# A Mamba block and a mixture of experts in one kernel: the statistics of z and the copies of last states on ScalarE, every engine's order rearranged

## The chip, the cores and the metric

The kernel runs on one core of a Trainium2 chip. Times are device microseconds (us) of one execution. A core has five engines that work through their own instructions in order and meet only at semaphores: TensorE (PE, with its weight loads as PEld), VectorE (DVE), ScalarE (ACT), GpSimd (POOL) and SyncE (SP, which issues all transfers here).

## The reference, cut to what matters

Four batches of 512 positions. Each goes through a selective state-space layer with 512 channels and 16 states per channel, gated by the layer-normed `x`, and then through a layer of 8 experts (the best 2 are weighted) and one shared expert.

```python
u = silu(causal_conv(in_proj_w @ ctx) + conv_b)
dt_lo, B, C = split(x_proj_w @ u)
delta = softplus(dt_proj_w @ dt_lo + dt_proj_b)
# for every position t
state = state * exp(delta_t * A) + delta_t * u_t * B_t
y_t = sum_over_states(state * C_t)
z = layernorm(x)                      # over 512
x = x + tanh(g_xattn) * (y + D * u) * silu(z)
n = layernorm(x)
top2 = top_k(softmax(n @ gate_w.T), 2)
h = gelu(n @ wd.T + bd) * weight_of_expert
x = x + tanh(g_ffn) * (h @ wu + bu + gelu(n @ ws_d.T + bs_d) @ ws_u.T + bs_u)
```

## The kernel before

**Units and slots.** The batches are cut into six units (`UNITS`): unit 0 and 1 are the halves of batch 0 (256 positions each), units 2 and 3 are batches 1 and 2 whole (512), units 4 and 5 the halves of batch 3. The recurrence of a unit is cut into slots, 128 in all: 16 in units 0, 1, 4 and 5, 32 in units 2 and 3. So unit 1 begins at slot 16, unit 2 at 32, unit 3 at 64, unit 4 at 96, unit 5 at 112. A slot holds 32 channels times 4 groups of states on 128 partitions and 1024 elements of states and positions. Four slots (`r` = 0 to 3) make up a group of 128 channels.

**One slot.** SP loads `dd` (delta and delta times u, spread over partitions). POOL multiplies by B for two slots at once into `ring` (`outers`, L988). ScalarE writes exp(delta A) into one of two PSUM buffers `decay` (`exps`, L1064), and may do so once the scan of two slots earlier, or its weighing, is done. VectorE runs the recurrence (`scan`, L1229). The multiplication by C is POOL's for r = 0 and 1 (`weigh`, L1010, two slots at once) and VectorE's for r = 2 and 3 (L1243, the result of the scan stays in `decay` until then). When a batch goes on in the next unit (units 0 and 4), the last states of a slot are copied into `carry`: by POOL for r = 0 and 1 (L1006), by VectorE for r = 2 and 3 (L1235, between scan and weighing). PE then sums over the states into `y_ps` (L1458; called y0.0 and so on: unit, then group). VectorE gates it with z (L1280), POOL adds the residual (L964). `ring` has ten buffers, so POOL's products for slot i wait until the sums up to slot i minus 10 are done.

**Preparation of a unit.** PE `in_proj` (L1474), ScalarE and VectorE the convolution (L1089, L1255, L1257), ScalarE SiLU (L1095), PE `x_proj` and `dt` (L1482, L1487), ScalarE softplus (L1115, with table loads around it), POOL delta times u (`du`, L957), SP's store and loads of `dd`.

**Statistics of z.** For each batch VectorE takes four times `bn_stats` and `bn_aggr` (L1270, L1272), POOL makes scale and shift of them (`affine_z`, L946 to L951), ScalarE applies SiLU (`silu_z`, L1099).

**The expert layer of a unit.** Means and variances over the channels by PE (`mean_p`, `mean`, `var_p`, `var`), centring and scaling by VectorE (L1305, L1311), the routing (L1344 to L1397), nine `down` jobs (L1523), read by ScalarE (L1163) and put through GELU in two pieces (L1170), eight `mix` jobs (L1527) that VectorE multiplies in (L1404), four `up` jobs (L1531, L1537) that VectorE reads (L1409). All these PE jobs share three PSUM banks `wk` in turn: a job waits until the bank's last reader is done. In this document "down5.0" is the first down job of unit 5.

**What sets the order.** Each engine's order is written down in the table `PLAN`: a number for each piece of work, in slots. PE and SP work through theirs sorted by number. On POOL, ScalarE and VectorE a piece is issued ahead of the slot whose number it has before the point, and the slots themselves follow a fixed loop. Nothing is decided at run time, and an engine that waits for one piece holds back all behind it.

## Time and profile before

| | us |
|---|---|
| median of 3 runs | 643.73 |
| the three runs | 643.26, 643.73, 643.81 |
| the profiled execution, its own time | 644.75 |
| its span, from the first instruction to the last | 643.0 |
| busy: PE, VectorE, POOL, ScalarE | 502.3, 505.0, 494.2, 396.6 |

The busy times are shares of the whole span, which has three parts: about 36 us until the first scan, the 128 slots until about 576 us, and an end of about 65 us in which PE works through the rest of the expert layers while POOL and, mostly, VectorE have nothing left. So an engine that is busy for 490 us is near its limit in the middle part. The profile attributes idle time to what ended it; where several semaphores are awaited that is the last one.

### The profile page before, as it was taken

To read this page: it belongs to the slowest core of one execution; us is meant where nothing else is said; L and a number is where in the kernel's file an instruction comes from. 1 tells how busy PE (TensorE), PEld (TensorE's weight loads), DVE (VectorE), ACT (ScalarE), POOL (GpSimd) and SP (SyncE) were. 2 spreads that over 40 slices of the span, in tenths; PEclk is the share of its full clock that TensorE was granted. 3 is DMA by queue.
4 is the path that set the end of the run, shared out by engine and by line. 5 is a ranking of instruction groups with operands and counts; after the bars stand their busy time and mean duration, and the time that the engine had idled before them with its cause. 6 is when DMAs were issued, how large, how long until landed. Compare 5 with 4: busy or idle time off the path is not lost.

```text
span 643.0 us, 7504 instructions
## 1 busy us (share of the span) xinstructions
PE 502.3 (78%) x2304; PEld 253.7 (39%) x2304; DVE 505.0 (79%) x560; ACT 396.6 (62%) x755; POOL 494.2 (77%) x240
## 2 busy tenths in 40 slices
PE   5605544787899698974399899974998999889988
PEld 4202211234564364610033333331443443657866
DVE  4477799878989999995879899958689879982211
ACT  4549656897926877474666854455689765681250
...
GB/s 83 166 371 210 255 66 99 115 249 166 97 150 184 63 196 2 106 113 304 244 95 7 130 79 110 27 240 201 50 49 41 208 181 123 25 2 67 33 1 49
DMA packets 39940, 79.70 MB, mean 124 GB/s; under 512 B 5977, under 2 KB 12761, under 8 KB 39900
## 3 DMA queue, kind: packets, MB, share of 16 engines
...
q8 instruction: 18, 0.29, 0.2%
q14 instruction: 22, 0.18, 0.1%
...
## 4 chain that ended last, share of the span: by engine, by line
DVE 34%; PE 27%; ACT 14%; issue 14%; POOL 7%; DMA 3%; ACTq 0%; DVEq 0%; SPq 0%; POOLq 0%
DVE decay L1229 11%; DVE ring L1229 8%; PE wk L1537 8%; PE wk L1523 7%; ACT decay L1064 5%; POOL ring L988 5%; DVE ring L1243 4%; PE y_ps L1458 3%; PE wk L1474 3%; DMA dd<-dd_scratch 2%; PE wk L1487 2%; ACT L1033 2%; POOL ring L1010 1%; DVE xc L1305 1%; ACT h L1163 1%
## 5 line engine op out<-in xcount | busy, mean ns | idle before, releaser
L988 POOL TENSOR_TENSOR ring<-dd,b_in 128x2048 f32<-128x2048 f32 x64 | 289.3, 4531 | 15.8 <-issue 13.1
L1064 ACT ACTIVATE decay<-dd,a_neg 128x255 f32<-128x255 f32 (+1 forms) x384 | 188.4, 533 | 37.3 <-DVE ring L1229 37.0
L1229 DVE TENSOR_TENSOR_SCAN ring<-decay,ring 128x1024 f32<-128x1024 f32 x64 | 144.4, 2277 | 16.1 <-ACT decay L1064 10.1
L1010 POOL TENSOR_TENSOR ring<-ring,c_in 128x2048 f32<-128x2048 f32 x32 | 144.9, 4527 | 13.1 <-DVE ring L1229 7.7
L1229 DVE TENSOR_TENSOR_SCAN decay<-decay,ring 128x1024 f32<-128x1024 f32 x64 | 146.3, 2285 | 8.5 <-ACT decay L1064 5.7
L1523 PE MATMUL wk<-xc,w_down 128*128 128x256 f32 (+1 forms) x432 | 139.4, 478 | 11.7 <-DVE xc L1311 6.0
L1537 PE MATMUL wk<-h,w_up 128*128 128x256 f32 (+1 forms) x432 | 137.2, 474 | 0.4 <-DVE h L1404 0.4
L1458 PE MATMUL y_ps<-ring,fold 128*32 128x256 f32 (+1 forms) x768 | 77.4, 547 | 64.3 <-DVE ring L1243 63.3
L1523 PEld LDWEIGHTS wk<-xc,w_down 128*128 128x128 f32 x432 | 84.3, 201 | 62.0 <-issue 46.6
L1537 PEld LDWEIGHTS wk<-h,w_up 128*128 128x128 f32 x432 | 84.3, 200 | 44.5 <-issue 35.1
L1243 DVE TENSOR_TENSOR ring<-decay,c_in 128x1024 f32<-128x1024 f32 x64 | 78.2, 1222 | 1.7
L1458 PEld LDWEIGHTS y_ps<-ring,fold 128*32 128x32 f32 x768 | 25.5, 127 | 109.2 <-DVE ring L1243 74.3
L1046 ACT ACTIVATE decay<-zeros 128x4 f32<-128x4 f32 (+1 forms) x64 | 10.9, 171 | 60.3 <-DVE ring L1243 60.2
L1474 PE MATMUL wk<-ctx_in,in_w 128*128 128x256 f32 (+2 forms) x96 | 40.4, 564 | 8.6 <-DMA ctx_in<-in_ctxT 6.3
L1163 ACT ACTIVATE h<-wk,b_down 128x256 f32<-128x256 f32 (+1 forms) x54 | 28.7, 538 | 26.3 <-PE wk L1523 26.2
L1409 DVE SCALAR_TENSOR_TENSOR x_out<-wk,consts,x_out 128x256 f32<-128x256 f32 (+1 forms) x24 | 13.5, 562 | 32.8 <-PE wk L1537 32.7
L964 POOL TENSOR_TENSOR x<-x,y_gated 128x256 f32<-128x256 f32 (+1 forms) x24 | 21.8, 910 | 18.4 <-DVE y_gated L1280 12.8
L957 POOL TENSOR_TENSOR dd_out<-dd_out,u 128x256 f32<-128x256 f32 (+1 forms) x24 | 21.4, 903 | 17.8 <-ACT dd_out L1115 17.6
L1404 DVE TENSOR_TENSOR h<-h,wk 128x256 f32<-128x256 f32 (+1 forms) x48 | 21.1, 501 | 14.1 <-PE wk L1527 13.1
L1487 PE MATMUL wk<-x_dbl,dt_w 16*128 16x256 f32 (+1 forms) x48 | 24.4, 630 | 9.9 <-DVE u L1255 5.6
L1255 DVE SCALAR_TENSOR_TENSOR u<-wk,conv_taps,u 128x255 f32<-128x255 f32 (+5 forms) x48 | 29.3, 613 | 3.6 <-ACT u L1089 2.4
L1474 PEld LDWEIGHTS wk<-ctx_in,in_w 128*128 128x128 f32 x96 | 21.0, 235 | 27.0 <-issue 20.4
...
## 6 DMA issues: line engine op xcount, KB each, us to landing
...
```

The lines of the kernel that those rows point to most:

```text
L988: nc.gpsimd.tensor_tensor(two, dd[:, j % DD_RING:j % DD_RING + 2, None, n:2 * n].broadcast_to([P, 2, TILES[v], n]), b_in[:, None, g % BC_R ...
L1010: nc.gpsimd.tensor_tensor(two, two, c_in[:, None, g % BC_RING].broadcast_to([P, 2, WIDE]), ALU.mult).then_inc(weighed_pool, 2)
L1064: last = nc.scalar.activation(decay[:, i % 2, q * n + 1:(q + 1) * n], dd[:, j % DD_RING, 1:n], ACT.Exp, scale=a_neg[:, c, r, k:k + 1])
L1163: nc.scalar.activation(h[:, k, columns(v)], wk[:, bank, 0:COLS[v]], ACT.Identity, bias=b_down[:, k:k + 1]).then_inc(drained[bank], 1)
L1229: last = nc.vector.tensor_tensor_scan(to, decay[:, i % 2], ring[:, i % RING], 0.0, ALU.mult, ALU.add)
L1243: nc.vector.tensor_tensor(ring[:, i % RING], decay[:, i % 2], c_in[:, g % BC_RING], ALU.mult).then_inc(weighed_dve, 1)
L1255: ins = nc.vector.scalar_tensor_tensor(to[:, d:], wk[:, bank, 0:n - d], tap, to[:, d:], ALU.mult, ALU.add)
L1458: last = nc.tensor.matmul(y_ps[r * BLOCK:(r + 1) * BLOCK, 0:n], fold[:], ring[:, slots[r] % RING, q * n:(q + 1) * n], start=False, stop=p ...
L1474: last = nc.tensor.matmul(wk[:, bank, 0:n + halo], in_w[:, j, k * P:(k + 1) * P], ctx_in[:, j, cols.start - halo:cols.stop], start=j == 0, ...
L1487: last = nc.tensor.matmul(o, dt_w[:, k * P:(k + 1) * P], x_dbl[0:R, 0:n], start=True, stop=True)
L1523: last = nc.tensor.matmul(o, w_down[:, j, k, :], xc[:, j, cols], start=j == 0, stop=j == NW - 1)
L1537: last = nc.tensor.matmul(o, w_up[:, j, k * P:(k + 1) * P], h[:, j, cols], start=False, stop=j == NE - 1)
```

## The change

Three things are changed.

1. **Statistics of z.** VectorE's `bn_stats` and `bn_aggr` go. ScalarE takes the sums by four copies of 128x512 in place with an accumulated sum (L1130 of after), the negative mean by one small copy (L1133), and the squares about the mean by eight squarings of 128x256 into a scratch tile with accumulated sums, each waiting for the one ahead (L1138). `affine_z` on POOL adds the two halves and divides; it has four small instructions as before.
2. **Copies of last states.** VectorE's copy for r = 2 and 3 goes, 16 in all. ScalarE makes it (`keep`) ahead of overwriting the `decay` buffer two slots later, so after the weighing; POOL's products of the next unit wait for it (`kept`).
3. **Order.** Every number of `PLAN` is new. Which instructions there are does not change by this. The identity matrix lies in `xc` during the constants' making, which frees memory for the scratch tile.

```diff
+Z_STEPS = 3 * NW + 1
     "z": [
-        [-1.66],
+        [-1.85],
...
-                pool.wait_ge(z_stats, 2 * NW * (b + 1))
+                pool.wait_ge(z_stats, Z_STEPS * (b + 1))
...
-                nc.gpsimd.tensor_tensor(z_ln[:, 0], z_mv[:, :, 1], eps.broadcast_to([P, NW]), ALU.add)
-                nc.gpsimd.tensor_tensor(z_ln[:, 1], z_mv[:, :, 0], minus_one.broadcast_to([P, NW]), ALU.mult).then_inc(z_scale, 1)
+                nc.gpsimd.tensor_tensor(z_ln[:, 0], z_var[:, :, 0], z_var[:, :, 1], ALU.add).then_inc(z_scale, 1)
+                pool.wait_ge(z_scale, 4 * b + 1)
+                nc.gpsimd.tensor_scalar(z_ln[:, 0], z_ln[:, 0], 1.0 / L, EPS, ALU.mult, ALU.add).then_inc(z_scale, 1)
...
+                    pool.wait_ge(kept, keeps(i + 1))
...
+            def keep(i):
+
+                v, c, p, r = PLACES[i]
+                if goes_on(v) and not weighs_on_pool(i):
+                    k, n = p * TILES[v], COLS[v]
+                    nc.scalar.activation(carry[:, c * NR4 + r, k:k + TILES[v], None],
+                                         decay[:, i % 2].rearrange("p (q n) -> p q n", n=n)[:, :, n - 1:n], ACT.Copy).then_inc(kept, 1)
...
+                    keep(i - 2)
                 reset(i)
+                if i > 1 and kept_of(i - 2):
+                    act.wait_ge(kept, kept_of(i - 2))
...
+            def stats_z(b, k):
+
+                pair = range(2 * (k % 2), 2 * (k % 2) + 2)
+                if k == 0:
+                    act.wait_ge(z_loaded, DMA * (b + 1))
+                    if b > 0:
+                        act.wait_ge(z_scale, 4 * b)
+                if k < 2:
+                    for c in pair:
+                        nc.scalar.activation(z[:, c, :], z[:, c, :], ACT.Copy, accum_out=z_sum[:, c:c + 1]).then_inc(z_stats, 1)
+                if k == 1:
+                    act.wait_ge(z_stats, Z_STEPS * b + NW)
+                    nc.scalar.activation(z_ln[:, 1], z_sum[:], ACT.Copy, scale=-1.0 / L).then_inc(z_stats, 1)
+                if k > 1:
+                    for c in pair:
+                        for half in range(2):
+                            act.wait_ge(z_stats, Z_STEPS * b + NW + 1 + 2 * c + half)
+                            nc.scalar.activation(z_scrap[:], z[:, c, half * L // 2:(half + 1) * L // 2], ACT.Square, bias=z_ln[:, 1, c:c + 1],
+                                                 accum_out=z_var[:, c, half:half + 1]).then_inc(z_stats, 1)
...
-                if goes_on(v) and not weighs_on_pool(i):
-                    steps[0] += 1
-                    last.then_inc(scan_step, 1)
-                    dve.wait_ge(scan_step, steps[0])
-                    k = p * TILES[v]
-                    last = nc.vector.tensor_copy(carry[:, j, k:k + TILES[v], None],
-                                                 to.rearrange("p (q n) -> p q n", n=n)[:, :, n - 1:n])
...
-                nc.vector.bn_stats(z_stat[:, c, :], z[:, c, :]).then_inc(z_stats, 1)
-                dve.wait_ge(z_stats, 2 * w + 1)
-                nc.vector.bn_aggr(z_mv[:, c, :], z_stat[:, c, :]).then_inc(z_stats, 1)
```

**Where rows move.** In the rows below a name such as `wk<-ctx_in,in_w` is what is written and what is read, the size is that of the output, and x8 stands for eight instructions in a row; what an instruction waits for stands in brackets.

The first place is the beginning of PE's order, before: `in_proj` of units 0 and 1 (`ctx_in`), `x_proj` (`xp_w`) and `dt` (`dt_w`) of unit 0, then the first sums.

```order
L1474 MATMUL wk<-ctx_in,in_w 128x256 x8
L1474 MATMUL wk<-ctx_in,in_w 128x259 x6
L1482 MATMUL wk<-u,xp_w 48x256 x4
L1487 MATMUL wk<-x_dbl,dt_w 128x256 x3
L1474 MATMUL wk<-ctx_in,in_w 128x259 x2
```

The same place after.

```order
L1498 MATMUL wk<-ctx_in,in_w 128x256 x8
L1506 MATMUL wk<-u,xp_w 48x256 x4
L1511 MATMUL wk<-x_dbl,dt_w 128x256
L1498 MATMUL wk<-ctx_in,in_w 128x259 x2
L1511 MATMUL wk<-x_dbl,dt_w 128x256 x3
```

Unit 1's `in_proj` (output 128x259) has moved behind `x_proj` and behind the first `dt`.

The second place is POOL between unit 3 and unit 4, before: from the last weighing of unit 3 (`c_in`) over `du` of unit 4 (`dd_out`) and unit 3's last residual (`x<-x,y_gated`) to unit 4's first products (`dd,b_in`) and `affine_z`.

```order
L1010 TENSOR_TENSOR ring<-ring,c_in 128x2048 [waits scanned,c_loaded2]
L957 TENSOR_TENSOR dd_out<-dd_out,u 128x256 [waits u_ready,drained2]
L957 TENSOR_TENSOR dd_out<-dd_out,u 128x256 [waits u_ready,drained0]
L957 TENSOR_TENSOR dd_out<-dd_out,u 128x256 [waits u_ready,drained1]
L957 TENSOR_TENSOR dd_out<-dd_out,u 128x256 [waits u_ready,drained0]
L964 TENSOR_TENSOR x<-x,y_gated 128x512 [waits gated]
L988 TENSOR_TENSOR ring<-dd,b_in 128x2048 [waits b_loaded0,dd_loaded5,summed,dd_loaded4]
L988 TENSOR_TENSOR ring<-dd,b_in 128x2048 [waits b_loaded0,dd_loaded1,summed,dd_loaded0]
L988 TENSOR_TENSOR ring<-dd,b_in 128x2048 [waits b_loaded0,dd_loaded3,summed,dd_loaded2]
L946 TENSOR_TENSOR z_ln<-z_mv,consts 128x4 [waits siluz_ready,z_stats]
```

The same place after, from the weighing but one of unit 3.

```order
L964 TENSOR_TENSOR dd_out<-dd_out,u 128x256 [waits u_ready,drained2]
L996 TENSOR_TENSOR ring<-dd,b_in 128x2048 [waits b_loaded0,dd_loaded5,summed,dd_loaded4]
L1018 TENSOR_TENSOR ring<-ring,c_in 128x2048 [waits scanned,c_loaded2]
L971 TENSOR_TENSOR x<-x,y_gated 128x512 [waits gated]
L996 TENSOR_TENSOR ring<-dd,b_in 128x2048 [waits b_loaded0,dd_loaded1,summed,dd_loaded0]
L971 TENSOR_TENSOR x<-x,y_gated 128x512 [waits gated]
L996 TENSOR_TENSOR ring<-dd,b_in 128x2048 [waits b_loaded0,dd_loaded3,summed,dd_loaded2]
L964 TENSOR_TENSOR dd_out<-dd_out,u 128x256 [waits u_ready,drained2]
```

Unit 4's first two products have moved ahead of unit 3's last residual, and its `du` are spread out: two are done before this place and in it, two come with the slots of unit 4.

The third place is the end of PE's order, before: from the sums of the last group, y5.3 (`y_ps<-ring,fold`), over unit 4's `up` (`w_up`) to unit 5's `down` (`w_down`) and `up`.

```order
L1458 MATMUL y_ps<-ring,fold 32x256 x16
L1527 MATMUL wk<-comb_parts,sel 128x256 x3
L1491 MATMUL wk<-x,consts 32x256 x4
...
L1531 MATMUL wk<-comb_parts,b_up 128x256
L1537 MATMUL wk<-h,w_up 128x256 x9
L1515 MATMUL wk<-ident,parts 48x128 x2
L1523 MATMUL wk<-xc,w_down 128x256 x28
L1527 MATMUL wk<-comb_parts,sel 128x256 x8
L1531 MATMUL wk<-comb_parts,b_up 128x256
```

The same place after.

```order
L1482 MATMUL y_ps<-ring,fold 32x256 x16
L1547 MATMUL wk<-xc,w_down 128x256 x8
L1515 MATMUL wk<-x,consts 32x256 x4
L1547 MATMUL wk<-xc,w_down 128x256 x4
...
L1547 MATMUL wk<-xc,w_down 128x256 x4
L1551 MATMUL wk<-comb_parts,sel 128x256 x3
L1555 MATMUL wk<-comb_parts,b_up 128x256
L1561 MATMUL wk<-h,w_up 128x256 x9
L1551 MATMUL wk<-comb_parts,sel 128x256 x5
L1555 MATMUL wk<-comb_parts,b_up 128x256
```

Four `down` jobs of unit 4 (16 matmuls) now stand behind y5.3, and unit 4's last `up` job stands between the third and the fourth `mix` job (`sel`) of unit 5.

## Rows read from the trace of the kernel before

**Rows 1.** the page: the chain that ended last, by engine.

```profile
DVE 34%; PE 27%; ACT 14%; issue 14%; POOL 7%; DMA 3%; ACTq 0%; DVEq 0%; SPq 0%; POOLq 0%
```

**Rows 2.** busy time by stretch: start:end, length, five engines, PE clock granted, DMA.

```profile
36.50:102.40 65.90, 24.66 (x148) 9.90 (x148) 57.22 (x52) 42.66 (x95) 62.88 (x31) 0.66 0.58 204
...
170.20:305.00 134.80, 110.48 (x528) 59.73 (x526) 122.01 (x131) 82.99 (x138) 119.40 (x38) 0.86 0.39 132
305.00:421.70 116.70, 100.33 (x353) 36.97 (x352) 109.54 (x96) 70.47 (x113) 109.17 (x33) 0.91 0.29 99
421.70:441.60 19.90, 11.46 (x46) 3.89 (x46) 12.76 (x23) 10.05 (x19) 15.37 (x6) 0.67 0.87 299
...
514.50:577.80 63.30, 57.62 (x364) 31.36 (x363) 55.87 (x58) 43.37 (x106) 55.61 (x31) 0.97 0.25 84
577.80:643.00 65.20, 59.77 (x271) 45.43 (x270) 15.12 (x46) 15.41 (x24) 0.73 (x1) 0.95 0.11 37
```

**Rows 3.** instructions by line and form: count, busy us, mean ns, idle before.

```profile
L988 POOL TENSOR_TENSOR ring<-dd,b_in 128x2048 f32<-128x2048 f32 x64 | 289.3, 4531 | 15.8 <-issue 13.1 <-DMA dd<-dd_scratch 2.7
...
L1270 DVE BATCH_NORM_STATS2 z_stat<-z 128x6 f32<-128x512 f32 x16 | 10.8, 672 | 0.0
...
L1272 DVE BATCH_NORM_AGGREGATE z_mv<-z_stat 128x2 f32<-128x6 f32 x16 | 2.9, 182 | 0.6
L1235 DVE COPY carry<-decay 128x4 f32<-128x4 f32 x16 | 2.6, 162 | 0.6
```

**Rows 4.** timeline of the beginning: start, length, engine, line, instruction, idle before.

```profile
22.62 1.22 PE L1487 MATMUL wk<-x_dbl,dt_w 16*128 16x256 f32 x2 [3.88 <-DVE u L1257]
23.88 0.47 ACT L1115 ACTIVATE dd_out<-wk,dt_bias 128x256 f32<-128x256 f32 x1 [3.28 <-PE wk L1487]
...
31.97 4.50 POOL L988 TENSOR_TENSOR ring<-dd,b_in 128x2048 f32<-128x2048 f32 x1 [1.36 <-DMA dd<-dd_scratch]
```

**Rows 5.** timeline on VectorE around the first statistics of z.

```profile
40.89 0.67 DVE L1270 BATCH_NORM_STATS2 z_stat<-z 128x6 f32<-128x512 f32 x1
...
44.07 2.28 DVE L1229 TENSOR_TENSOR_SCAN decay<-decay,ring 128x1024 f32<-128x1024 f32 x1
```

**Rows 6.** instructions by line and form on ScalarE.

```profile
L1033 ACT ACT_TABLE_LOAD x24 | 30.8, 1283 | 0.4
...
L1099 ACT ACTIVATE z<-z,z_ln 128x512 f32<-128x512 f32 x16 | 11.7, 803 | 4.9 <-POOL z_ln L951 4.8
...
L1095 ACT ACTIVATE u<-u 128x256 f32<-128x256 f32 x16 | 5.3, 401 | 0.0
...
L1170 ACT ACTIVATE h<-h 128x2560 f32<-128x2560 f32 x2 | 4.7, 2341 | 0.0
...
L1095 ACT ACTIVATE u<-u 128x512 f32<-128x512 f32 x8 | 4.4, 616 | 0.0
```

**Rows 7.** timeline between unit 3 and unit 4.

```profile
427.49 1.27 POOL L964 TENSOR_TENSOR x<-x,y_gated 128x512 f32<-128x512 f32 x1 [3.21 <-DVE y_gated L1280]
...
428.71 13.50 POOL L988 TENSOR_TENSOR ring<-dd,b_in 128x2048 f32<-128x2048 f32 x3
...
441.62 2.27 DVE L1229 TENSOR_TENSOR_SCAN ring<-decay,ring 128x1024 f32<-128x1024 f32 x1
...
453.76 2.30 DVE L1229 TENSOR_TENSOR_SCAN decay<-decay,ring 128x1024 f32<-128x1024 f32 x1 [4.03 <-ACT decay L1064]
```

**Rows 8.** timeline of the end, on PE.

```profile
604.03 12.46 PE L1523 MATMUL wk<-xc,w_down 128*128 128x256 f32 x56
...
620.78 6.68 PE L1537 MATMUL wk<-h,w_up 128*128 128x256 f32 x18 [0.36 <-DVE h L1404]
...
627.60 4.15 PE L1537 MATMUL wk<-h,w_up 128*128 128x256 f32 x18
```

**Rows 9.** busy time by stretch at the end.

```profile
620.80:627.50 6.70, 6.70 (x19) 5.20 (x19) 0.00 (x1) 0.00 (x0) 0.00 (x0) 0.62 0.00 0
627.50:640.40 12.90, 12.84 (x57) 10.20 (x56) 1.47 (x4) 0.00 (x0) 0.00 (x0) 1.00 0.16 51
```

572 lines of the change are left out of this document (285 added, 287 removed), and 77 rows, old and new, of the table PLAN.

## The prediction

> **What bounds the kernel now.** I read four views in this order: the page's chain, the busy time by stretch, the groups of instructions, and the timeline where the change moves something. In the chain no engine leads: VectorE has 34%, PE 27%, ScalarE 14%, issue 14% and POOL 7% [rows 1]. The stretches [rows 2] say where each one counts. In unit 0 POOL is busy 62.88 of 65.9 us and VectorE 57.22. In unit 2 it is VectorE, 122.01 of 134.8, with POOL at 119.40; in unit 3 they are level, 109.54 and 109.17 of 116.7. In unit 5 PE is the busiest, 57.62 of 63.3, VectorE and POOL just behind. In the last 65.2 us PE alone counts, 59.77. ScalarE is the bound in none of them, at 57% to 69% of a stretch. Between units 3 and 4 there is a hole: from 421.7, where the slots of unit 3 are through, to the next scan at 441.62 [rows 2, 7] nobody is full. That is 19.9 us without a scan.
>
> The profiled execution took 644.75, 1.02 above the median of 643.73. I add up differences on its span of 643.0 and apply the sum to the median; that both scale alike is an assumption, and 0.16% of the sum is nothing. About 0.2%, or 1.3 us, is what a measurement of this kernel can tell from no change.
>
> **Part 1, the statistics.** VectorE is rid of 16 times 672 plus 182 ns [rows 3], 13.7 us, 3.4 for each batch; by the starts of the first statistics and of the scan behind them, 40.89 and 44.07, a set takes 3.2 [rows 5]. ScalarE gets four copies of 128x512, a small one and eight squarings of 128x256 for each batch, all with an accumulated sum, which no row shows. Bounds for the copy: 616 ns is 128x512 with a plain scale, 803 the one with two operands per partition [rows 6]; for the squaring 401 from below [rows 6] and, since every one waits for the one ahead and stores its sum, 401 plus 162 plus a wait, say 0.7, from above. I take 0.75 and 0.55: 4 x 0.75 + 0.2 + 8 x 0.55 = 7.6 for each batch, 30 in all (bounds 23 and 37). So the same work costs ScalarE over twice what VectorE saves. It is free where ScalarE has slack over the slots around it, as in unit 2 (83 of 134.8 busy), and it is not where a set stands as a block ahead of an `exps`: there are only two `decay` buffers, so ScalarE is never more than two slots ahead.
>
> The trace has ScalarE's 128x512 at 616 to 803 ns against VectorE's pair at 854, so per instruction there is no loss; it is the second pass that doubles the cost. The Trainium skill, "ScalarE: Activation LUTs", section "Rules for kernel authors", tells one to put adds and multiplies on VectorE and not on ScalarE, which speaks against this part. Its section "What ACT_TABLE_LOAD costs" gives 186 + 0.833 N ns with immediates and some 93 more per pointer operand: as an estimate 0.61 for the copy and 0.49 for the squaring, 6.4 a batch instead of my 7.6, with no figure for the accumulated sum. By that price the sum stays at 634.2, since I count the statistics as hidden; by the rule as written the part would be a loss, the rival further down that gives 650. No row here shows either yet.
>
> **Part 2, the copies of last states.** VectorE loses 16 times 162 ns and the wait for the scan's end ahead of each, together some 3.3 us, all in units 0 and 4 [rows 3]. ScalarE gets 16 small ones in place of them, about 0.2 each. They come ahead of overwriting `decay`, two slots later, for which the weighing had to be finished anyway, so they add no wait but only their length and that of the semaphore behind them: 0.3 to 0.5 us in a slot of about 4 (134.8 us for 32 slots in unit 2 [rows 2]). POOL's wait for them comes at the next unit's products, long after. I put the part at nothing by itself; it counts in what VectorE gains below.
>
> **Part 3, the order, by stretch.** *Beginning and unit 0.* PE's first `dt` stood 3.88 us waiting for a bank that VectorE's convolution of unit 1 held [rows 4]: unit 1's `in_proj` had been queued ahead of it. Now it comes behind, so the softplus (which had waited 3.28 for PE), the store and POOL's first product follow earlier: 31.97 becomes about 28, if the wait of 1.36 for the transfer stays [rows 4]. Unit 0 is bound by POOL, whose work in it does not change, so the gain is carried through to slot 16. Next in line is the first set of statistics: it now takes 7.6 of ScalarE between two `exps` where VectorE lost 3.2, and may eat some of the gain. I take **-4.0**, bounds -5.5 and 0.
>
> *Units 1 to 3.* Unit 2 gives VectorE 3.2 back, and its slack is 134.8 - 122.0 = 12.8, POOL's 15.4: both engines have idle time from waits on each other, so the gain can't be larger than what VectorE loses plus some of these. I take **-3.0**, bounds -4.5 and +1.5 (the last when ScalarE's 7.6 hold an `exps`). In unit 3 VectorE also loses 3.2 us of statistics, but gets part of unit 5's convolution, about as much, so 0; unit 1 gets no statistics before or after: 0.
>
> *The hole.* POOL waits 3.21 us for the gate of unit 3's last group, y3.7, takes the residual (1.27) and only then three products, 13.5 us [rows 7]; the first scan of unit 4 needs the first of them, and the loads of unit 4 (DMA busy share 0.87 in this stretch [rows 2]) had to be there. VectorE meanwhile has 12.76 us of other work [rows 2], mostly a convolution, a centring and statistics that stand there in one lump. After, the first products of unit 4 are ahead of the last residual, in part before unit 3's last weighing, and `dt` and convolution are spread over the units on either side. If everything then were ready, the next scan could follow within a slot (about 4 us) instead of 19.9: the upper end is -16. But the work of the stretch is still to be done: VectorE's 12.76 less 3.2 of statistics, POOL's 15.37, ScalarE's 10.05 plus 7.6 for statistics [rows 2]. Where it's put now, in slots 96 to 108, ScalarE is the one that is full: softplus for unit 5, its table loads of 1283 ns each, silu(z) at 803 x 4 and the statistics come in the same eight or nine slots. Even so slot 108 should come some 14 us sooner. At slot 112 both pieces of unit 4's GELU are now near each other, each with a table load ahead and one behind: twice 1.28 + 2.34 + 1.28 = 9.8 at most [rows 6], and the reads of the down jobs beside them. `exps` of slots 113 to 116 wait for that, with VectorE's and POOL's work behind them; this gives back about 9. That leaves -5; POOL, which enters unit 5 with less behind it (55.61 of 63.3 busy, so 7.7 to spare), gives 2 more. I take **-7.0**, bounds -16 and -1. The wait for `decay` shows today already, 4.03 us in one slot of unit 4 [rows 7]; it is what is late next.
>
> *The end.* From the last group y5.3 on, PE is the bound. Unit 5's last four down jobs have been moved behind it. 56 records, seven jobs, take 12.46, so 1.78 each [rows 8]: 7.1, and with `comb` and three mixes about 8.2 of PE work that used to run beside the slots. Against this, unit 4's last `up` now stands between the mixes of unit 5 and covers the wait for the last GELU. There PE had been idle enough for the granted clock to fall: the up job at 620.78 took 6.68 at a granted 0.62 (near 1.2 GHz through much of it), the one at 627.60 took 4.15 at 1.00 (2.4 GHz) [rows 8, 9]. Keeping the clock gives 2.5, the waits about 1.2. Net **+4.5**, bounds +2 (PE has only 5.7 us to spare in unit 5, so these jobs were not wholly hidden before and give part of it back there) and +8.4 (nothing of the clock and the waits is saved).
>
> **The sum.** -4.0 - 3.0 - 7.0 + 4.5 = -9.5. On the median: 643.7 - 9.5 = **634.2**. All low ends together would give 620, all high ones 653. Half of each distance, added in squares since the terms are independent, is 4.8 downward and 4.7 upward: the forecast's own range is 629 to 639.
>
> **Rivals.**
> *The hole closes nearly entirely.* ScalarE's extra in slots 96 to 108 is taken up in its slack (31% to 43% idle in the stretches above), the bunch at slot 112 costs 3 and not 9, and the sum gains 6 to 8 more: 627. For it: ScalarE idles 9.85 of 19.9 us in the hole [rows 2]. Against: its work stands in lumps, and there are two buffers only.
> *POOL sets the pace and VectorE's relief is worth nothing.* POOL does 64 products of 4.53 us [rows 3], none less after, and is at 89% to 95% in units 0, 2 and 3 [rows 2]. What the hole gains by starting early is then lost again before slot 112, because POOL's products there are as many as before. What is left is the beginning, -4.0, and the end at its upper value, +8.4, less perhaps 1 to 3 of the hole: **646**, slower. It decides if POOL's idle time between slot 96 and y5.3 shrinks by less than 4 us.
> *ScalarE becomes the bound.* If statistics and copies cost their upper bounds (37 + 8 = 45 us) and two thirds of a set are each time ahead of an `exps` that VectorE awaits, four sets cost 4 x 5 = 20, VectorE's 3.2 x 4 come back only if it isn't waiting, and the order's gain of 14 is used up: about **650**. Against: ScalarE's 57% to 69%. In this case the rule of the Trainium skill that is named above, in "ScalarE: Activation LUTs", would prove right.
> *The change does only half of it:* the hole halves, the end gives it back, and the time is within 1.3 of before, 643.7.
>
> **Chances.** Forecast 0.55; the hole closes 0.18; POOL 0.13; ScalarE 0.06; the half-done change 0.08. So faster by over 0.2%: 0.73; within 0.2%: 0.08; slower by over 0.2%: 0.19. The range for 8 in 10 reaches from 624, which holds most of the larger gain, to 646, which ends at POOL's case and leaves ScalarE's out.
>
> **What would show it.** *Beginning:* POOL's first product near 28, no wait of PE ahead of the first `dt`, slot 16 near 98.5. *Statistics:* ScalarE's busy time up by 30, to some 428, VectorE's down by 16, to about 489; squarings near 0.55 and copies near 0.75. *Hole:* the first scan of unit 4 within 5 us of the last slot of unit 3, then scans that wait for `decay`; another, shorter standstill after slot 112. *End:* y5.3 to the end about 70 us instead of 65, with the last up jobs all at 4.15 and clock 1.00. I am wrong if the time up to slot 96 does not drop by 5 to 8 us, if the wait for `decay` grows beyond some 25 us over the whole run, or if the end grows by more than 8.

## The result, and the profile after

The changed kernel took 625.3 us (median of 4 executions, 617.63 to 629.19), against 643.77 before (643.26 to 644.36). These medians stand 18.5 us apart, a ratio of 0.971; the two quicker of the four, 617.63 and 622.23, count as fast runs and alone give 0.963 (95% interval 0.957 to 0.969). Six more executions gave 626.33 (623.04 to 628.71) against 643.9, ratio 0.972 (0.970 to 0.975). So the change makes the kernel some 18 us faster, nearly twice the 9.5 that was forecast. That is below the forecast's own range of 629 to 639, and just inside the low end of the one for 8 in 10, 624 to 646. The changed kernel also scatters over 11.6 us in its first four executions and 5.7 in the six, where the one before stays within 4.2 in eleven. The profile shown is that of the quickest of the six, 623.04 us with a span of 621.3, so some 4 us of the 21.7 between the two spans are scatter.

Busy time by stretch, with the same borders as [rows 2]: unit 0, unit 1, unit 2, unit 3 up to slot 92, slots 92 to 112, unit 5 up to the end of y5.3, the end.

```profile
37.50:96.40 58.90, 26.85 (x160) 10.71 (x160) 51.77 (x37) 49.41 (x123) 57.44 (x27) 0.67 0.68 226
96.40:160.40 64.00, 46.81 (x284) 25.00 (x284) 60.26 (x67) 55.16 (x122) 62.41 (x34) 0.85 0.41 140
160.40:282.30 121.90, 105.95 (x480) 60.21 (x484) 113.72 (x112) 88.55 (x160) 119.90 (x38) 0.83 0.43 147
282.30:394.40 112.10, 96.48 (x338) 35.11 (x330) 101.05 (x91) 79.01 (x142) 106.85 (x33) 0.85 0.36 126
394.40:490.00 95.60, 85.25 (x397) 35.02 (x396) 76.66 (x78) 77.33 (x170) 79.45 (x40) 0.95 0.37 127
490.00:547.90 57.90, 54.41 (x298) 27.02 (x296) 52.90 (x44) 34.36 (x89) 51.08 (x27) 0.97 0.30 101
547.90:621.30 73.40, 67.12 (x312) 51.31 (x308) 18.01 (x61) 23.51 (x36) 0.72 (x1) 0.97 0.10 33
```

Three stretches of the kernel before that [rows 2] do not show by themselves: unit 1, unit 3 up to slot 92, and slots 92 to 112.

```profile
102.40:170.20 67.80, 53.91 (x282) 27.48 (x282) 57.05 (x60) 56.09 (x119) 64.13 (x34) 0.76 0.50 168
305.00:411.00 106.00, 90.54 (x309) 33.10 (x309) 98.88 (x89) 64.32 (x104) 99.32 (x28) 0.90 0.31 106
411.00:514.50 103.50, 86.55 (x352) 35.33 (x351) 83.09 (x97) 73.72 (x138) 77.86 (x38) 0.85 0.36 123
```

The chain that ended last, against [rows 1]:

```profile
PE 30%; DVE 26%; ACT 19%; issue 16%; DMA 4%; POOL 3%; SPq 1%; DVEq 0%; ACTq 0%; POOLq 0%
```

ScalarE has 19% of it instead of 14%, VectorE 26% instead of 34%. In unit 2 POOL is busy 119.90 of 121.9 us; it was 119.40 of 134.8 [rows 2]. POOL's work in it has hardly changed, its idle time is nearly gone. The prediction's terms side by side with the lengths of the stretches:

| stretch | before | after | change | forecast |
|---|---|---|---|---|
| until the first scan, and unit 0 | 36.5 + 65.9 | 37.5 + 58.9 | -6.0 | -4.0 |
| unit 1 | 67.8 | 64.0 | -3.8 | 0 |
| unit 2 | 134.8 | 121.9 | -12.9 | -3.0 |
| unit 3 up to slot 92 | 106.0 | 112.1 | +6.1 | 0 |
| slots 92 to 112 (the hole, and what follows) | 103.5 | 95.6 | -7.9 | -5.0 |
| slot 112 to y5.3 | 63.3 | 57.9 | -5.4 | -2.0 |
| the end | 65.2 | 73.4 | +8.2 | +4.5 |
| sum | 643.0 | 621.3 | -21.7 | -9.5 |

A second profile of the changed kernel, of an execution of 628.36 us with a span of 626.6, tells scatter from effect. There the first two rows are -2.5 and -2.8, unit 2 -14.1, unit 3 up to slot 92 +4.8, slots 92 to 112 -4.8, and all from slot 112 on +3.0. Unit 2 stands out in both; the size of the head's gain does not hold.

ScalarE's `exps` and VectorE's scans by line, then the new instructions on ScalarE by line and form (count, busy us, mean ns, idle before):

```profile
L1088 ACT ACTIVATE decay<-dd,a_neg 128x255 f32<-128x255 f32 (+1 forms) x384 | 188.4, 533 | 27.7 <-DVE ring L1271 27.4
L1271 DVE TENSOR_TENSOR_SCAN decay<-decay,ring 128x1024 f32<-128x1024 f32 x64 | 145.8, 2285 | 15.8 <-ACT decay L1088 14.5
...
L1138 ACT ACTIVATE z_scrap<-z,z_ln 128x256 bf16<-128x256 f32 x32 | 16.2, 506 | 0.9
L1130 ACT ACTIVATE z<-z 128x512 f32<-128x512 f32 x16 | 9.8, 616 | 0.2 <-DMA z<-in_x 0.2
L1138 ACT ACTIVATION_READ_ACCUMULATOR z_scrap<-z,z_ln 128x1 f32 x32 | 6.0, 187 | 0.0
L1130 ACT ACTIVATION_READ_ACCUMULATOR z<-z 128x1 f32 x16 | 3.0, 187 | 0.0
L1067 ACT ACTIVATE carry<-decay 128x4 f32<-128x4 f32 x16 | 2.6, 162 | 8.1 <-DVE ring L1278 8.1
```

An accumulated sum is an instruction of its own, 187 ns, that overlaps its neighbour a little. A set from 38.4 to 46.1 us (in the run head_fix3) is 7.7 us, the 7.6 of the prediction; ScalarE's busy time rose from 396.6 to 426.2, VectorE's fell from 505.0 to 488.5. These terms were right in size. For the set that is in part luck: from start to start a copy with its sum takes 0.61 us where 0.75 was taken, and a squaring with its sum 0.64 where 0.55 was, and the two errors cancel.

### The profile page after: what moved, and what is told of

It reads as the page before. It is cut to its first block, busy times and chain, and to the rows that moved or that the text cites. A ratio compares the mean times of both kernels' runs of the same rounds, so it can differ in the third digit from the quotient of the medians.

```text
span 626.6 us, 7564 instructions
## 1 busy us (share of the span) xinstructions
PE 499.8 (80%) x2304; PEld 253.7 (40%) x2304; DVE 487.9 (78%) x512; ACT 426.5 (68%) x872; POOL 494.0 (79%) x240
## 4 chain that ended last, share of the span: by engine, by line
DVE 30%; PE 29%; ACT 17%; issue 13%; DMA 7%; POOL 3%; SPq 1%; DVEq 0%; ACTq 0%; POOLq 0%
DVE ring L1271 10%; DVE decay L1271 9%; PE wk L1547 8%; PE wk L1561 8%; ACT decay L1088 5%; DVE ring L1278 3%; PE y_ps L1482 3%; DMA dd<-dd_scratch 3%; DVE u L1290 2%; POOL ring L996 2%; PE wk L1511 2%; ACT z_scrap L1138 2%; PE wk L1523 2%; PE wk L1498 2%; PE wk L1506 2%
## 5 line engine op out<-in xcount | busy, mean ns | idle before, releaser
L1088 ACT ACTIVATE decay<-dd,a_neg 128x255 f32<-128x255 f32 (+1 forms) x384 | 188.4, 533 | 27.2 <-DVE ring L1271 26.9
L1561 PE MATMUL wk<-h,w_up 128*128 128x256 f32 (+1 forms) x432 | 134.9, 468 | 1.6 <-DVE h L1430 1.5
L1561 PEld LDWEIGHTS wk<-h,w_up 128*128 128x128 f32 x432 | 82.4, 195 | 45.4 <-issue 36.6
L1482 PE MATMUL y_ps<-ring,fold 128*32 128x256 f32 (+1 forms) x768 | 73.3, 523 | 11.3 <-POOL ring L1018 5.7
L1506 PE MATMUL wk<-u,xp_w 128*48 128x256 f32 (+1 forms) x48 | 20.7, 590 | 25.7 <-ACT u L1119 24.7
L964 POOL TENSOR_TENSOR dd_out<-dd_out,u 128x256 f32<-128x256 f32 (+1 forms) x24 | 21.8, 914 | 21.3 <-ACT dd_out L1159 21.2
L1498 PEld LDWEIGHTS wk<-ctx_in,in_w 128*128 128x128 f32 x96 | 21.7, 240 | 31.5 <-issue 17.4
```

The costliest lines, as they stand in the source:

```text
L1088: last = nc.scalar.activation(decay[:, i % 2, q * n + 1:(q + 1) * n], dd[:, j % DD_RING, 1:n], ACT.Exp, scale=a_neg[:, c, r, k:k + 1])
L1482: last = nc.tensor.matmul(y_ps[r * BLOCK:(r + 1) * BLOCK, 0:n], fold[:], ring[:, slots[r] % RING, q * n:(q + 1) * n], start=False, stop=p ...
L1498: last = nc.tensor.matmul(wk[:, bank, 0:n + halo], in_w[:, j, k * P:(k + 1) * P], ctx_in[:, j, cols.start - halo:cols.stop], start=j == 0, ...
L1506: last = nc.tensor.matmul(o[0:R + 2 * NS, :], xp_w[:, j, :], u[:, (NW * v + j) % U_RING, 0:n], start=j == 0, stop=j == NW - 1)
L1561: last = nc.tensor.matmul(o, w_up[:, j, k * P:(k + 1) * P], h[:, j, cols], start=False, stop=j == NE - 1)
```

## Experiments: order and engines apart

**The changed kernel again**, unchanged.

> The changed kernel again, unchanged: its four runs so far lie between 617.6 and 629.2, at mean granted TensorE clocks from 0.895 down to 0.861, where the kernel before stays within 1 us. If the clock is what spreads them, the runs go on lying on one line of time against clock (about 3 us for 0.01) and the profile of a quicker run shows the same stretches until some stretch in which PE is the busiest, with a higher granted clock there. If it is something else (transfers, POOL), the clock would be the same over quick and slow runs in the stretches that differ.

Measured: 626.33, six executions at mean granted clocks from 0.865 to 0.871, with times from 623.04 to 628.71 that do not follow the clock. The first four had followed it, from 617.63 at 0.895 to 629.19 at 0.861. So the clock as a whole does not explain the scatter of the six, and for the first four that is open. Two profiles, 626.6 and 621.3 long, differ by 1.6 us at slot 0, by 3.8 at slot 8, by 1.7 to 5.9 from there to slot 108 and by 5.1 at slot 112. In the longer one PE's clock was 0.62 against 0.70 in the stretch from 39 to 75 us, and VectorE waited 2.1 us for a y's sums (0 in the other). What starts it was not tried.

**The order alone.** The code of before with the new `PLAN`.

```diff
 PLAN = {
-    (numbers of before)
+    (numbers of the changed kernel)
 }
```

> Kernel before with the numbers of the changed kernel's table and nothing else: statistics and copies stay on VectorE. Theory 1 (the order is the gain, POOL's 15 us of idle time in unit 2 and the hole are what closes): -12 to -18 against before, about 628. Theory 2 (VectorE's relief is the gain, the order only serves it): -2 to -6, about 640, since VectorE is given 16 us back in places where it is full.

Measured: 630.70 (630.04 to 632.68), ratio 0.980 (0.977 to 0.982), -13.2. Three quarters of the gain need no change of engines. By stretches: unit 0 58.5, unit 1 64.5, unit 2 122.6, unit 3 up to slot 92 115.0, slots 92 to 112 98.6. Against the changed kernel it lacks mainly 2.9 and 3.0 us in the last two.

**The engines alone.** The changed code with the numbers of before.

> Changed kernel with the numbers of the table of before: statistics and copies on ScalarE, old order. Theory 1 (order): within 3 us of before, 641 to 646, as the lump of VectorE at slot 35 only moves to ScalarE, whose four pieces of 7.6 us stand ahead of an exps. Theory 2 (VectorE's relief): -8 or more, below 636. Theory 3 (statistics on ScalarE hurt where they stand in one slot): slower than before by 3 to 10.

Measured: 679.33 (678.71 to 681.16), ratio 1.055 (1.052 to 1.058): 35 us slower than before. None of the theories had that. By the slots' starts it is lost in four places, where the sets stand: 4.8 us in slots 0 to 4, 5.9 in 32 to 36, 5.9 in 64 to 68 and 15.1 in 92 to 100. ScalarE's waits in the stretch around slot 35, and its timeline before slot 96:

```profile
ACT z L1128 <- DMA z<-in_x: 5.5, 1, 5.5
```

```profile
454.67 0.63 ACT L1128 ACTIVATE z<-z 128x512 f32<-128x512 f32 x1 [10.47 <-DMA z<-in_x]
```

VectorE, in the same kernel around slot 96 and around slot 35:

```profile
456.49 1.52 DVE L1290 SCALAR_TENSOR_TENSOR u<-wk,conv_taps,u 128x256 f32<-128x256 f32 x3 [9.73 <-ACT u L1111]
460.94 1.52 DVE L1290 SCALAR_TENSOR_TENSOR u<-wk,conv_taps,u 128x256 f32<-128x256 f32 x3 [2.93 <-ACT u L1111]
467.63 1.52 DVE L1290 SCALAR_TENSOR_TENSOR u<-wk,conv_taps,u 128x256 f32<-128x256 f32 x3 [5.17 <-ACT u L1111]
```

```profile
197.11 2.32 DVE L1288 SCALAR_TENSOR_TENSOR u<-wk,conv_taps,u 128x511 f32<-128x511 f32 x3 [11.40 <-ACT u L1111]
```

ScalarE runs up to two slots ahead of VectorE. With the same slot number it meets the statistics earlier, when z is not loaded yet, and waits 5.4 us in slot 2, 5.5 in slot 35, 10.5 in slot 96, with its reads of PE's banks and its `exps` queued behind. VectorE then waits for those reads. In the kernel before VectorE, which comes last, took the same statistics without any wait for the transfer.

The third set is different. ScalarE meets it in slot 67 with z already there, and does it as one block of 7.7 us. The reads of the means' chain stand behind it, and VectorE waits for them with its scans behind. ScalarE and VectorE there:

```profile
319.69 0.61 ACT L1128 ACTIVATE z<-z 128x512 f32<-128x512 f32 x1
```

```profile
336.83 2.29 DVE L1335 TENSOR_TENSOR xc<-xc,wk 128x2048 f32<-128x2048 f32 x1 [10.64 <-ACT wk L1180]
```

In the kernel before VectorE waited 1.51 us at this place. So the block costs 5.9 us here with no transfer awaited.

**The statistics spread.** As the engines alone, with the four pieces of a set in different slots.

```diff
-stats_z: 2.2 2.4 2.6 2.8 | 35.5 35.625 35.75 35.875 | 67.286 67.429 67.571 67.714 | 96.667 96.75 96.833 96.917
+stats_z: 2.2 2.6 3.2 3.6 | 35.5 36.5 37.5 38.5 | 65.5 66.6 67.5 68.5 | 96.9 97.2 98.1 98.5
-affine_z: 0.667 | 36.5 | 66.5 | 98.5
+affine_z: 2.5 | 39.5 | 68.6 | 98.5
```

> As engines_alone (679.3), but the four pieces of each set of statistics stand in two to four slots instead of in one, and POOL's affine_z behind them. If the block of 7.6 us between two exps is what costs (4.7 to 5.9 us in slots 0 to 4, 32 to 36, 64 to 68 and 12 to 15 around slot 96 in the run of engines_alone), a third to two thirds of the 35 us come back: 655 to 668. If the price is ScalarE's 30 us as such or POOL's wait for affine_z, nothing comes back: 675 to 682.

Measured: 673.47 (672.11 to 674.66), ratio 1.044, -5.9 of the 35, between the two expectations. Slots 32 to 36 came back to 22.5 us from 28.7 (before: 22.8), although ScalarE still waited for z there:

```profile
186.12 0.63 ACT L1128 ACTIVATE z<-z 128x512 f32<-128x512 f32 x1 [5.85 <-DMA z<-in_x]
```

Slots 64 to 68 came back to 21.2 from 26.4 (before: 20.5). So in slots 32 to 36 the block was what cost. In 64 to 68 that is less sure, since a long wait had moved just ahead of them: the third set's first piece, now in slot 65, waited 12.4 us for z, with the read that unit 4's convolution needs behind it, and slots 60 to 64 took 28.7 us instead of 20.4. ScalarE's waits for z grew from 21.4 us in all to 29.6, so the total does not measure the block alone.

**The statistics later, still in a block.**

```diff
-stats_z: 2.2 2.4 2.6 2.8 | 35.5 35.625 35.75 35.875 | 67.286 67.429 67.571 67.714 | 96.667 96.75 96.833 96.917
+stats_z: 3.3 3.5 3.7 3.9 | 37.6 37.7 37.8 37.9 | 68.7 68.8 68.9 68.95 | 98.1 98.3 98.5 98.7
-affine_z: 0.667 | 36.5 | 66.5 | 98.5
+affine_z: 4.2 | 38.5 | 68.6 | 98.6
```

> As engines_alone (679.3), but each set of statistics stands later in ScalarE's order, where z has been loaded, still as one block in one slot: slots 3, 37, 68 and 98 instead of 2, 35, 67 and 96. In engines_alone ScalarE waited 5.4, 5.5 and 10.5 us for the transfer of z with all its exps behind, in engines_spread 12.4 at slot 65. If these waits are most of the price, 650 to 662. If the block of 7.6 us itself is, it stays at 670 to 680.

Measured: 668.12, ratio 1.036 (1.033 to 1.038), -11.2 (-13.1 between the two profiles). Slots 32 to 36 took 18.6 us, 10.1 less than with the engines alone, and slots 92 to 96 took 32.2 against 42.6. The wait for z was 0.4 us there instead of 5.5, and 4.0 instead of 10.5. But in the head the set now met another wait: ScalarE stood 7.3 us for POOL's `affine_z` ahead of SiLU, slot 4 came at 65.1 instead of 61.0, and slots 0 to 4 took 5.0 us more. Slots 64 to 68, where there had been no wait for z, stayed at 27.2. So where the waits for the load shrank, 20.5 us came back, and 7.4 were lost elsewhere, 5.0 of them to the next wait in the head. Load and block do not add up: in slots 32 to 36 either edit alone took the whole loss away. The shares of the two in the 35 us stay open.

**The statistics back on VectorE**, in the new order.

> Changed kernel with the statistics back on VectorE as before, copies on ScalarE, new order. Theory 1: +1 to +5 against the changed kernel (VectorE 13.7 us more, of which most lies in its idle time). Theory 2: +8 to +14. If ScalarE's 30 us are the costlier place: 0 or faster than the changed kernel.

Measured: 629.54, ratio 0.978 (0.975 to 0.980), +3.2 against the changed kernel, as theory 1 had it. With the order alone at 630.70, the copies of last states are worth some 1.2 us, no more than the scatter. That the statistics gain 3 us in this order and stand among the losses in the old one fits their places: here z is there when ScalarE comes (a wait of 0.2 us in all), and three of the four sets are spread over two to four slots.

## Experiments: where the order gains

**The new order from a slot on.** Three kernels with the code of before; an entry keeps its old number if both numbers lie below the border.

> Code of before (statistics and copies on VectorE); every entry of the table whose number is below 20 in both tables keeps before's number, all others get the changed kernel's. By the starts of the slots in the run of the new order alone (-5.2 us at slot 16, -1.4 at slot 20, -13.6 at the end), the part up to slot 20 gives next to nothing: 630 to 634. If the head's gain counts in full, it is lost here: about 636.

> The same with the border at 45. The slots say that the order gains 16 us between slots 20 and 44. If these are independent of what follows, they are lost here and the later order by itself gives +3 to +6 against before: 647 to 650. If the later order gains by itself, through the hole, as the prediction had it (-7 and +4.5): about 641.

> The same with the border at 65, so the order of before up to unit 3, then the new one: the hole between units 3 and 4 closes, unit 3 and slots 100 to 112 get longer, the end gets longer. By the slots of the order alone against before from slot 64 on (345.1 against 338.0 us): +7, so about 650. The prediction's terms for this part, -7.0 and +4.5, would give 641.

Measured: 653.44, 645.56 and 645.02 (ratios 1.015, 1.000 and 1.001). From 65 on, the stretches from slot 64 to 92, 92 to 112, and from there to the end:

```profile
299.90:413.70 113.80, 92.90 (x322) 33.93 (x314) 103.71 (x99) 71.17 (x114) 106.61 (x33) 0.85 0.34 120
413.70:512.10 98.40, 86.55 (x396) 35.30 (x395) 81.18 (x93) 69.75 (x138) 79.21 (x40) 0.93 0.35 124
512.10:643.80 131.70, 121.87 (x605) 78.28 (x603) 70.91 (x104) 58.00 (x124) 52.08 (x28) 0.97 0.19 63
```

Slot 64 comes 5.0 us sooner than before, slot 96 16.6 sooner: the hole is closed. But unit 3 up to slot 92 takes 113.8 us against 106.0, and slot 112 comes only 2.4 sooner; the end takes that and 0.8 more. From slot 64 on it is 343.9 us against 338.0. Closing the hole is worth nothing by itself in this kernel: its work is in the slots on either side. The border at 20 has a fault of its own: ahead of slot 20 a centring waits 15.9 us for PE, whose means wait for a residual that POOL does late, and 20 us are lost. But from there on the pieces add up to the microsecond: slots 20 to 64 take 169.8 us, with the whole new order 169.4, before 188.7; from slot 64 on it is 345.1 in both. So the order's gain is made in unit 1 and unit 2, 19 us, the first 20 slots give 1.4, and all from unit 3 on costs 7. Of unit 2's 134.8 us 129.1 are left with the border at 65, 130.1 at 45, 122.6 with the whole: some 5 are saved by what is moved out of its end into unit 3, the rest by what is ordered below 45. The kernels with borders at 45 and 65 end level with before, within 0.2%. Their expectations had 647 to 650 and about 650, or 641 by the theory of the hole, so both are misses. Which rows of the order make the gain in units 1 and 2 was not found: none of the single moves that follow brings it.

**One place at a time, in the kernel before.** VectorE's lumps at slots 35 and 44:

```diff
-stats_z: 35.5 35.625 35.75 35.875    affine_z: 36.5
+stats_z: 36.6 37.6 38.5 39.6         affine_z: 40.5
-shares: 44.75    comb: 44.42    comb read: 46.5
+shares: 46.25    comb: 46.1     comb read: 47.45
```

> Kernel before with two groups of VectorE's work in unit 2 spread and nothing else: the statistics of batch 1 from slot 35 over slots 36 to 39 (POOL's affine_z behind them), and the end of the routing of unit 1 with its PE job from slot 44 to 46. If the lumps are what unit 2 loses (a scan 9.4 us late at slot 35, 7.7 us of POOL idle before slot 44), unit 2 shrinks by 4 to 8 us from 134.8, and the total by as much less what comes back later: 637 to 641. If VectorE's load as such is the bound in unit 2, nothing changes: 643 to 645.

Measured: 653.47, 9 us slower. Slot 36 came no sooner: VectorE waited for PE's up jobs there, 2.1 and 1.6 us, where it had waited 2.0 us and then done the statistics in the kernel before. So the lump had filled time that is idle without it. The loss itself came in slots 44 to 48, 7.6 us: ScalarE, which reads `comb` in its order ahead of an `exps`, stood still for PE:

```profile
243.66 0.38 ACT L1154 ACTIVATE comb_parts<-wk 48x256 bf16<-48x256 f32 x1 [7.90 <-PE wk L1512]
```

The weighing ahead of the routing (`weigh_d` 44.5 to 44.1), and the reads of unit 0's up jobs a slot later (`up read` 35.375, 36.333, 37.5 to 36.05, 36.6, 37.7, SP's transfers likewise):

> Kernel before with one number changed: VectorE's weighing in slot 44 stands ahead of the routing of unit 1 (13 small instructions, 2.9 us) and not behind it. In the trace of before, the weighing at 227.3 releases the exps at 228.7, their end at 230.0 releases SP's load, and that POOL's product at 233.9, which POOL had waited 7.7 us for. If this chain is what POOL waits for, the wait shrinks by 2 to 3 us to about 5, and slot 48 comes 2 to 3 us sooner; total 641 to 643. If POOL waits for something else, nothing changes (643.3 to 645).

> Kernel before with three of VectorE's four reads of unit 0's up jobs put a slot later (behind the scan of slot 35), and SP's transfers for them. In the trace of before, the first read waited 2.0 us for PE ahead of that scan, and with the convolution and the statistics the scan came at 189.3 where the one ahead had begun at 177.6. If the read's place costs, slots 36 to 40 come 2 to 4 us sooner: 640 to 642. If the wait only moves to the next scan or to PE (its banks are held longer), 643 to 647.

Measured: 644.16 and 643.81 against 644.82, ratios 0.999 (0.998 to 1.001) and 0.999 (0.998 to 1.000), so no difference that can be told. With the weighing first POOL waited 8.0 us there instead of 7.7: ScalarE's `exps` stood behind the routing's exponential and the reads of down jobs, not behind the weighing. With the reads later slot 36 came 3.5 us sooner as expected, and slot 64 still 1.8, but 1.3 of both were there at slot 32, ahead of the edit.

The gate at the border of units 2 and 3:

```diff
-gate y2.7: 64.5    conv 4.3: 64.75    residual 2.3: 62.5
+gate y2.7: 66.5    conv 4.3: 66.6     residual 2.3: 64.5
```

(the last of the four columns each; the residual is that of y2.7)

> Kernel before with three numbers changed: VectorE's gate of y2.7 and the convolution of unit 4's last 128 channels stand behind the scans of slots 64 and 65 and not ahead of them, POOL's residual behind one more product. In the trace of before the first scan of unit 3 began at 304.96, though POOL's product and ScalarE's exps were there by 299.7: VectorE waited 3.77 us for PE's sums and 0.87 for ScalarE's read, and did 2.3 us of work. If that is the cause, slot 64 comes 4 to 5 us sooner. If the gain lasts, the total is 639 to 641; if the wait is met again behind (PE's means wait for this residual), slot 72 shows less than 1 us of it and the total is 643 to 645.

Measured: 648.69, ratio 1.005 (1.004 to 1.007). Slot 64 came 3.5 us sooner, slot 68 2.8 later, slot 84 5.3 later. VectorE in this kernel behind the first scans of unit 3:

```profile
305.89 0.73 DVE L1277 SCALAR_TENSOR_TENSOR y_gated<-y_ps,consts,z 128x512 f32<-128x512 f32 x1
312.12 2.29 DVE L1302 TENSOR_TENSOR xc<-x,wk 128x2048 f32<-128x2048 f32 x1 [5.51 <-PE wk L1496]
```

The gate feeds the residual, that PE's means, and the centring, number 66.5 on VectorE as before, waited 5.5 us for them with all scans behind it. The gain moved from one wait into a longer one. The changed kernel moves the whole chain at once: `mean read` to 67.667, `scale_x` to 70.5, the statistics to 70.7 and later.

The residual on which the prediction laid the hole (number 92.875 to 94.5):

> Kernel before with POOL's last residual of unit 3 behind unit 4's first product instead of ahead of it. The prediction held that this residual (3.2 us of waiting for the gate, 1.27 of work) keeps unit 4's first scan late. If so, slot 96 comes 3 to 4.5 us sooner than 441.6 and the total drops by 1 to 4. If VectorE's lump of other work (12.8 us of the 19.9) is what keeps it late, slot 96 does not move, and the chain of means starts later: total 644 to 648.

Measured: 648.36, ratio 1.005 (1.003 to 1.006). POOL's product began at 425.98 instead of 428.71, but the first scan of unit 4 came at 445.14, 3.5 us later than before. VectorE ahead of it:

```profile
427.94 1.53 DVE L1254 SCALAR_TENSOR_TENSOR u<-wk,conv_taps,u 128x256 f32<-128x256 f32 x3 [0.17 <-ACT u L1086]
436.34 1.52 DVE L1254 SCALAR_TENSOR_TENSOR u<-wk,conv_taps,u 128x256 f32<-128x256 f32 x3 [6.87 <-ACT u L1086]
438.26 2.29 DVE L1302 TENSOR_TENSOR xc<-x,wk 128x2048 f32<-128x2048 f32 x1 [0.40 <-PE wk L1496]
...
445.14 2.27 DVE L1226 TENSOR_TENSOR_SCAN ring<-decay,ring 128x1024 f32<-128x1024 f32 x1
```

It was never the product that was awaited. The queue of convolutions, centring and statistics ahead of the scan was, and in it the chain over residual and means.

**What takes the hole's gain back.** Half of unit 3's down jobs:

```diff
-for j in range(NW):
+for j in range(2 if v == 3 else NW):
     last = nc.tensor.matmul(o, w_down[:, j, k, :], xc[:, j, cols], ...)
```

> Changed kernel with the work of unit 3's nine down jobs halved (two of the four blocks of channels are left out, 18 matmuls of 128x512, some 16.6 us of PE). It asks why the hole that was closed between units 3 and 4 is paid back in slots 100 to 112, where PE is busy 95% in the changed kernel. If PE is the bound there, slot 112 comes 8 to 15 us sooner and the total falls by about as much. If ScalarE (table loads, GELU, softplus) or the chain from the last residual over the means to the first down job is the bound, slot 112 moves by under 4 us.

Measured, one execution: 626.61; slots 100 to 112 took 71.3 us against 70.3, where 8 to 15 less were expected if PE is the bound. PE is not the bound there, though it is 92% busy. Its records say why less work hardly left idle time: from 467 to 490 us, with the down jobs halved on the first row and whole on the second (the changed kernel),

```profile
467.00:490.00 23.00, 18.66 (x99) 6.57 (x98) 17.63 (x15) 20.07 (x37) 20.97 (x11) 0.72 0.25 88
```

```profile
467.90:490.00 22.10, 20.82 (x127) 8.35 (x126) 17.04 (x17) 20.78 (x39) 19.70 (x12) 1.00 0.14 48
```

the granted clock fell from 1.00 (2.4 GHz) to 0.72, between the two levels. ScalarE is busy 20 to 21 of 22 to 23 us in both. That it and the waits around it are the bound fits, but was not shown by taking its work away.

## Experiments: the head

In the changed kernel the first `dt` no longer waits, but the fourth does, and POOL's last `du` with it, ahead of the first product:

```profile
26.55 1.22 PE L1511 MATMUL wk<-x_dbl,dt_w 16*128 16x256 f32 x2 [2.58 <-DVE u L1292]
```

```profile
30.83 0.73 POOL L964 TENSOR_TENSOR dd_out<-dd_out,u 128x256 f32<-128x256 f32 x1 [5.55 <-ACT dd_out L1159]
31.52 13.44 POOL L996 TENSOR_TENSOR ring<-dd,b_in 128x2048 f32<-128x2048 f32 x3
```

The product began at 31.52, not near 28 as forecast. Three edits of the changed kernel followed.

```diff
-in_proj 1.0: -3.82    in_proj read 1.0, 1.1: 0.769 0.846
+in_proj 1.0: -2.4     in_proj read 1.0, 1.1: 0.93 0.94
```

> Changed kernel with in_proj1.0 moved behind dt0.3 on PE, and its read behind that of dt0.3 on ScalarE. The fourth dt of unit 0 then no longer stands behind the bank that VectorE's convolution holds, POOL's du0.3 comes some 4 to 5 us sooner, and so does POOL's first product (31.5 to 33.1 before the edit, 26 to 28 with it). If nothing else is late there, the total drops by 4 to 5 to about 621. The rival: ScalarE meets the statistics of batch 0 after two exps and waits for z's load, which ended at 38.4 in one profile, so slot 2 comes as late as before the edit and the total moves by less than 1.5.

Measured: 635.26, 9 us slower. The product began at 30.66, but VectorE's split of the biases now ran beside it:

```profile
30.61 0.41 DVE L1315 CAST b_up<-h 51x512 bf16<-51x512 f32 x1
31.05 4.88 DVE L1316 TENSOR_TENSOR h<-h,b_up 51x512 f32<-51x512 f32 x1
35.96 4.61 DVE L1317 TENSOR_SCALAR h<-b_up,part_mask 51x512 f32<-51x512 bf16 x1
40.61 4.60 DVE L1318 CAST b_up<-h 51x512 bf16<-51x512 f32 x1
45.25 0.68 DVE L1319 TENSOR_TENSOR h<-h,b_up 51x512 f32<-51x512 f32 x1
```

```diff
 (as head_fix, and)
-biases: 0.667
+biases: 0.5
```

> As head_fix (in_proj1.0 behind dt0.3), but with VectorE's split of the biases moved ahead of its convolution of unit 1, into the 10 to 11 us in which VectorE waits for ScalarE there. In head_fix three instructions of the split ran beside POOL's first products and took 4.88, 4.61 and 4.60 us instead of 0.68, 0.48 and 0.42, and slot 0 came at 50.4. If POOL's instructions hold them up, all seven take 4.2 us together here, slot 0 comes at 35 to 36 and the total is 10 or more below head_fix, at about 625. If these three are slow for another reason (where they stand after ScalarE or PE), they stay at over 4 us wherever they are put, and the total stays above 632.

Measured: 626.26. The same instructions, with POOL idle:

```profile
15.42 0.68 DVE L1316 TENSOR_TENSOR h<-h,b_up 51x512 f32<-51x512 f32 x1
16.14 0.48 DVE L1317 TENSOR_SCALAR h<-b_up,part_mask 51x512 f32<-51x512 bf16 x1
16.65 0.42 DVE L1318 CAST b_up<-h 51x512 bf16<-51x512 f32 x1
...
45.77 2.30 DVE L1269 TENSOR_TENSOR_SCAN decay<-decay,ring 128x1024 f32<-128x1024 f32 x1 [7.45 <-ACT decay L1086]
```

That the three instructions wait for POOL is shown: 0.68, 0.48 and 0.42 us against 4.88, 4.61 and 4.60, about the length of one product. Slot 0 now begins at 33.9, 3.6 sooner, and slot 2 at 45.8 as ever, since ScalarE waits for z and then does the statistics. The total is that of the changed kernel. At last the statistics behind slot 2 (`stats_z` 3.43 to 3.86, `affine_z` 4.3):

> As head_fix2 (626.3, slot 0 at 33.9, but slot 2 at 45.8 as ever), with ScalarE's statistics of batch 0 moved behind the exps of slot 2, into slot 3. If they were what held slot 2, it comes at about 38.5, slot 4 some 3 to 4 us sooner than 56.0, and the total is 622 to 624. If POOL's work (it has 62 us in unit 0) or the wait for the set moved to slot 4 gives it all back, slot 16 stays at 96 to 98 and the total at 625 to 628.

Measured: 626.42. Slot 2 came at 38.8, so the statistics had held it. But slot 4 came at 57.0, not 3 to 4 us sooner than 56.0: VectorE waited 5.1 us for `c_in`'s transfer and 4.7 for a `decay`, slot 16 at 98.9. No version beat the changed kernel.

## Why the prediction was wrong, point by point

**The step that failed is the bound on unit 2.** "The gain can't be larger than what VectorE loses plus some of these": -3.0, no lower than -4.5. It was -12.9 (-12.2 with the order alone, so hardly any of it is VectorE's relief). The rows for a wider bound were there: POOL idle for 15.4 of 134.8 us and VectorE for 12.8 [rows 2]. I took these as given, though a new order acts on just this. It left POOL 2.0 us. Part of the length went into unit 3, +6.1 where 0 stood: VectorE's busy time in unit 2 fell by 8.3 us, 3.4 of them statistics and about 3 the last two convolutions of unit 4, which I counted nowhere. Net, units 2 and 3 gave 6.8. Unit 1 gave 3.8 more (3.4 with the order alone), where I had put 0 only because it has no statistics; POOL is its busiest engine, with 64.13 of 67.8 us. For units 1 to 3 together -10.6 stands against -3.0, and this is the larger part of what the forecast missed.

**The head** was near in size (-6.0 for -4.0, -2.5 in the other profile) by luck, and wrong in mechanism: the first product came 0.45 us sooner, not 4, slot 0 came 1.0 us later, and the gain arose inside unit 0, 65.9 to 58.9, where POOL's idle time went from 3.0 to 1.5 and its work in the stretch from 62.9 to 57.4. I followed one of four `dt`, and not POOL's `du` that stands in the queue ahead of the product.

**The hole** was right in sign and within its bounds: -7.9 for -5.0 over slots 92 to 112 and -5.4 for -2.0 in unit 5, with a give-back as foreseen: slot 96 came 35.9 us sooner than before, slot 112 24.5. Its cause was named wrongly (residual_later), and it is no gain of its own (order_from_65): without the new order of the slots ahead it ends at zero.

**The end** was mis-sized: +8.2 for +4.5, just under my upper bound of +8.4. PE's busy time rose by 7.4 us, near what the moved jobs and mixes cost; the savings hardly came. One up job still ran at a low clock, now the first behind y5.3: 5.84 us, at a granted 0.76 from 561 to 568 us, after PE had waited 1.4 us. The later ones took 4.12 to 4.15 with the clock at 1.00. Against the 6.68 of [rows 8] that gives back 0.8 of the 2.5, and PE's idle time in the end rose from 5.4 to 6.3 us instead of falling by 1.2. The prediction calls the moved jobs unit 5's; they are unit 4's.

**Statistics and copies** were right: 7.7 us a set, the sign, and the small net (4.4 us for both). The copy took 0.616 us and the squaring 0.506, each with 0.187 for its sum. The estimates 0.61 and 0.49 from the 186 + 0.833 N ns of the Trainium skill, "ScalarE: Activation LUTs", section "What ACT_TABLE_LOAD costs", agree with the first two, and the section has no figure for the third. (The 6.4 a batch worked out of them leaves the small copy out, which makes it 6.6.) The rule in that page's "Rules for kernel authors", to put adds and multiplies on VectorE and not on ScalarE, would have been the better advice in the old order (679.33 against 643.9, the copies moved too) and not in the new one (626.33 against 629.54).

**The rivals.** The nearest number was that of the rival at 627, the hole closing nearly entirely, which had 0.18. That is luck too: the hole did close, but the gain did not come from it (order_from_65), and slots 100 to 104 alone took 16.3 us of it back. That ScalarE becomes the bound, priced at 650, is real at 679 once the old order is kept; what made it so was the set's place, as a block and ahead of its transfer, not the upper cost of the work. The case against it was read too well: the stretches shown have ScalarE at 60% to 69%, not 57% to 69%, and unit 1 at 83% (56.09 of 67.8). POOL as the pace-setter was right as a fact, and my conclusion from it wrong: POOL at 89% of unit 2 left 11% to be had.

**The signs.** Of the three that were to show the forecast wrong, two came true: slot 96 came 35.9 us sooner, where 5 to 8 was to be the gain up to it, and the end grew by 8.2, where 8 was the limit. VectorE's waits for `decay` grew from 15.8 to 21.5 us only.
